# Head-size-8 cross attention without the unread products of steps 5, 7 and 9

## The reference

```python
def _attn(x, ctx, wq, wk, wv, wo, bo, heads):
    b, n, _ = x.shape
    j = ctx.shape[1]
    dh = wq.shape[1] // heads
    scale = dh ** (-0.5)
    q = (x @ wq).reshape(b, n, heads, dh).transpose(0, 2, 1, 3)
    k = (ctx @ wk).reshape(b, j, heads, dh).transpose(0, 2, 1, 3)
    v = (ctx @ wv).reshape(b, j, heads, dh).transpose(0, 2, 1, 3)
    sim = jnp.einsum('bhid,bhjd->bhij', q, k) * scale
    a = jax.nn.softmax(sim, axis=-1)
    out = jnp.einsum('bhij,bhjd->bhid', a, v)
    out = out.transpose(0, 2, 1, 3).reshape(b, n, heads * dh)
    return out @ wo + bo
h1 = _ln(x, n1_g, n1_b)
x = _attn(h1, h1, q1, k1, v1, o1_w, o1_b, heads) + x
h2 = _ln(x, n2_g, n2_b)
x = _attn(h2, context, q2, k2, v2, o2_w, o2_b, heads) + x
```

## Time and profile before

| | us |
|---|---|
| median of 3 runs | 3592.56 |
| lowest and highest | 3588.77, 3592.84 |
| the profiled execution | 3591.85 |
| its span, first to last instruction | 3590.0 |

### The profile page before, as it was taken

The page is one execution under the profiler, slowest core; times in us unless marked ns, Lnnn a source line. Parts: engine busy times, 40 slices in busy tenths (PEclk is TensorE's granted clock), DMA queues, the critical chain, the costliest instruction groups (busy, mean ns, idle before and its releaser), DMA issues. The chain is left out here.

```text
span 3590.0 us, 93153 instructions
## 1 busy us (share of the span) xinstructions
PE 3523.7 (98%) x37535; PEld 3076.2 (86%) x37535; DVE 2304.3 (64%) x3902; ACT 2078.7 (58%) x5150; POOL 1254.3 (35%) x1278
## 2 busy tenths in 40 slices
PE   8999999999999999999999999899999999999999
PEld 6777777877887999999999999788888888888888
DVE  5888866664454676676667667566666666666554
ACT  4777777775335666565656656455555555555343
POOL 4433333332442433333333333333322332233432
PEclk9999999999999999999999999999999999999999
DMA  4444433231001000000000000100000000000000
GB/s 104 112 113 99 107 77 95 77 91 56 21 0 36 2 1 2 2 1 2 2 2 1 2 2 2 27 3 3 4 3 4 3 3 4 3 3 1 20 22 22
DMA packets 99741, 101.46 MB, mean 28 GB/s; under 512 B 31248, under 2 KB 74128, under 8 KB 99344
## 3 DMA queue, kind: packets, MB, share of 16 engines
q1 hardware_dynamic: 93408, 94.41, 10.3%
q0 software_dynamic: 5120, 1.35, 0.2%
q10 hardware_dynamic: 816, 0.08, 0.0%
HBM read 20.76 MB, written 5.24 MB: 7 GB/s over the span
## 5 line engine op out<-in xcount | busy, mean ns | idle before, releaser
L1217 POOL TENSOR_TENSOR a_probs<-a_probs,a_rsums 128x1024 f32<-128x1024 f32 x160 | 303.7, 1898 | 709.1 <-DVE a_rsums L1346 707.1
L1249 ACT ACTIVATE a_probs<-a_scores_banks,a_negmax 128x128 f32<-128x128 f32 x1280 | 372.5, 387 | 197.4 <-DVE a_negmax L1325 197.4
L1729 ACT ACTIVATE c_probs<-c_scores_banks,c_negmax 128x77 f32<-128x77 f32 x1280 | 317.5, 350 | 251.7 <-DVE c_negmax L1836 251.6
L1691 POOL TENSOR_TENSOR c_probs<-c_probs,c_rsums 128x616 f32<-128x616 f32 x160 | 197.7, 1236 | 725.0 <-DVE c_rsums L1848 724.9
L731 ACT ACTIVATE s_probs<-s_scoresT_banks 128x1024 f32<-128x1024 f32 (+1 forms) x320 | 327.4, 1023 | 182.8 <-PE s_scoresT_banks L908 180.5
L817 DVE TENSOR_REDUCE s_negmax<-s_scores_banks 128x8 f32<-128x1024 f32 (+1 forms) x320 | 322.3, 1007 | 134.6 <-PE s_scores_banks L890 130.5
L1354 DVE COPY a_probsT<-a_scores_banks 128x1024 f32<-128x1024 f32 x160 | 195.7, 1223 | 169.7 <-PE a_scores_banks L1422 169.6
L2230 DVE SCALAR_TENSOR_TENSOR f_hidden<-f_value_bank,bias,f_gate 128x512 f32<-128x512 f32 x160 | 120.0, 750 | 245.2 <-ACT f_gate L2205 243.2
L686 POOL DMA_DIRECT2D s_q_stack<-s_shift x160 | 93.6, 585 | 490.2 <-ACT s_shift L754 483.8
L2205 ACT ACTIVATE f_gate<-f_gate_bank,bias 128x512 f32<-128x512 f32 x160 | 110.0, 688 | 259.8 <-PE f_value_bank L332 259.7
L1853 DVE COPY c_probsT<-c_pt_banks 77x1024 f32<-77x1024 f32 x160 | 194.5, 1216 | 77.1 <-PE c_pt_banks L1929 77.1
(11 more groups left out here) (309 smaller groups left out, 10349.5 us busy)
## 6 DMA issues: line engine op xcount, KB each, us to landing
s_q_stack<-front SPq DMA_DIRECT2D x192, 160.0 KB, 3.3
s_k_stack<-front SPq DMA_DIRECT2D x96, 160.0 KB, 3.8
s_out<-s_heads SPq DMA_DIRECT2D x128, 80.0 KB, 2.5
s_k_stack<-front SPq DMA_DIRECT2D x96, 96.2 KB, 2.8
x_tokens<-in_x SPq DMA_DIRECT2D x16, 320.0 KB, 3.7
out_x<-x_tokens SPq DMA_DIRECT2D x16, 320.0 KB, 2.4
s_q_stack<-s_shift POOLq DMA_DIRECT2D x160, 8.0 KB, 2.5
s_ctx_in<-in_ctx SPq DMA_DIRECT2D x16, 115.5 KB
```

What stands on the lines that cost most here:

```text
L1217: nc.gpsimd.tensor_tensor(probs[n % 4][:], probs[n % 4][:], rsums[n % 2][:].unsqueeze(2).broadcast_to([P, UNIT, TOK]), ALU.mult).then_inc( ...
L1249: last_one = nc.scalar.activation(probs[n % 4][:, h, :], scores[n % 2][:, h // GROUP, h % GROUP * TOK:(h % GROUP + 1) * TOK], ACT.Exp, bia ...
L1691: nc.gpsimd.tensor_tensor(probs[i][:], probs[i][:], rsums[(k - 1) % 2][:].unsqueeze(2).broadcast_to([P, UNIT, NK]), ALU.mult).then_inc(s_p ...
L1729: done = nc.scalar.activation(probs[i][:, h, :], scores[:, h // GROUP, h % GROUP * NK:(h % GROUP + 1) * NK], ACT.Exp, bias=negmax[k % 2][: ...
```

## The change

The table `KEEP` loses its entries for the steps 5, 7 and 9:

```diff
@@ -489,7 +489,7 @@
     HALF = D // 2
     SPREAD = 4
     ST_LAG, PV_LAG = 5, 6
-    KEEP = {2: 3, 4: 3, 5: 4, 6: 3, 7: 4, 8: 6, 9: 4}
+    KEEP = {2: 3, 4: 3, 6: 3, 8: 6}
     BURST, BURST_QUADS = 12, (18, 23, 28)
     CONSTANTS, CONSTANTS_ALL = 8, 17
     START, START_KEEP = 10, 4
```

## The result

The changed kernel takes 3797.4 us in the median (3780.57 to 3832.99, 4 runs) against 3592.7 us before: a ratio of 1.0578, with an interval of 1.0533 to 1.0622. The forecast was 3575.5 us. Leaving out 188 products that nobody reads costs 205 us.

A forecast was written before the change was run, and what follows sets the result against it. TensorE's own work was taken to bound the kernel. Steps 5 and 7 were to give 16.6 us and step 9 0.5, so 3592.56 - 17.1 = 3575.5 us, with a range of 3568 to 3592.

The forecast's parts named there:

- What bounds the kernel: Cross attention, 450 to 850 us: TensorE's own work sets the pace, busy 397.22 of 400 us, except at one wait.
- The price of four products: Four unread products in a step of the cross attention: 0.52 us by their starts, 0.13 us each.
- Steps 5 and 7: Cross-attention quads: nothing takes the place of the removed time in these two steps, 32 x 0.52 = 16.6 us gained.
- rival (d): Steps 6 and 8: removed time returns as waits for ScalarE or VectorE; 3584 us if half is lost; chance 0.10.
- Step 9: End of the quad: transposes wait for ScalarE's copy, so no gain in 14 quads, about 0.5 us in the fifteenth group.
- The clock: End of step 9, 0.7 us of waiting: at most two drops in the likeliest case, 1.56 us each.
- two rivals: Clock drops at step 9 in some quads, 3580 to 3592.5 us, chance 0.25; or twice per quad, 3625 us, 0.08.
- Rival (b): Clock drops twice per quad, at step 9 and between steps 5 and 8: 32 x 1.56 = 50 us, 3625 us; chance 0.08.
- The point of decision: Clock drops in the cross attention: break-even at 11, slower by over 0.2% from 16 on, one per quad.
- The range: Whole kernel's time: from full gain, 3568 us, to eleven drops of the clock, 3592 us.

## Why the prediction was wrong

**What bounds the kernel**: right. TensorE sets the pace, and at full clock the time follows its instructions.

**The price of four products**: 0.52 us was read from starts; the step got 0.45 shorter, since the product behind them costs 0.07 more when it follows the products with the values directly. The estimate from the Trainium skill's weight load, 0.43 us for four by "TensorE: Matmul & The Clock Gate", section "LDWEIGHTS (loading the stationary operand)", comes closer to this net price than my reading did. No run here shows that the loads set it.

**Steps 5 and 7**: 1.04 us per quad forecast, 0.75 measured (25.27 to 24.52). Besides the 0.07 twice, the steps 6 and 8 lose 0.15 us, in step 8 to ScalarE's copy of the heads. I had checked that copy against ScalarE's own next task, but not against TensorE's products with the values, which wait for it. This is rival (d) in small. With the products of step 9 kept, the gain was 14.2 us in the median, against the 16.6 forecast for these two steps; its interval just includes none.

**Step 9**: right that its products hide in the wait and give no time; the wait went to 0.64 us. This is where the reasoning stopped short. A piece of work that costs nothing can still be what holds the clock.

**The clock**: the step that failed. The sum of 3575.5 puts the loss of the clock at nothing, on the ground that the place lies between a case that fell and one that didn't. In the cross stage that term came to about 213 us. The place was named (the end of step 9 as the barest), and given 0.33 in two rivals with a price of 1.56 us per fall and a break-even at 11 falls. The profiled execution has five in the stage, and they cost 213 us. The price per microsecond was about right, 1.56 / 3.41 = 0.46 against 0.42. The mis-sized term is the length: I took the 3.4 us of the one fall that I had looked at the earlier trace rows, which ended at once, for the length of any. Both falls in the earlier trace rows are that long, so nothing there warned. The falls at the changed place last 51 to 307 us, since the stage at half clock wins the clock back only now and then. The second error was to ask for gaps. The prediction weighed a wait of 0.7 us against one of 1.83. The run with 31-row products fell with TensorE busy for 99.8% of the time ahead of it. The prediction also read the Trainium skill ("TensorE: Matmul & The Clock Gate", section "HAM oscillation — how this bites in real kernels") as leaning against the change. The waits of the kernel that the Trainium skill tells of there are DMA waits of about 3 to 5 us, far longer than the 0.64 us here, so it bore less on the case than that. And the wait of 0.55 us at 446.74, in the trace of before, was a case nearer than those of the earlier trace rows.

**Rival (b)**, slower, was right in sign and wrong in its mechanism: not two short falls in each quad but a few long ones. The point of decision was wrong with it: at 0.42 us for each microsecond one fall of 41 us takes the forecast gain of 17.1.

**The range** went from full gain to eleven short falls. With what the runs showed it should have held two separate cases: about 3592.7 - 12 = 3581 us if the clock holds, and the measured 3781 to 3833 if it doesn't.

## What to carry to other kernels

Before taking work off TensorE that "only" keeps it warm, ask for each place whether the work stands in the barest piece of the loop, and test removals one place at a time: here the four products that were free in time were needed to hold the clock, and of the eight that cost time ten executions showed no need. Needed isn't the same as enough: with seven products in step 9 and none in the even steps three of four executions lost the clock. Price a loss of the clock with two cases, held and lost, and not as a count of short falls: a stage that only just holds the full clock need not win it back at half. Look at the granted clock by stretches; the busy share was 98% in both kernels.

## What the runs showed of the hardware that was not expected

- TensorE stayed at 1.2 GHz for up to 369 us while it was busy for all of the time (368.60 of 368.60), in the variant with bursts in step 5.
- Four products on 31 of 128 rows, of the same length in time as full ones (0.67 and 0.68 us for four), don't hold the clock where the full ones do: 3758 us against 3593.
- In the changed kernel the falls of the stage begin within 2 us behind the start of the transposes. The long ones end 10 to 12 us behind the transposes that begin a slow quad, where the projections run, but not in every quad, and the last of them ends with the stage; why one ends after 10 us (in the variant with two products in step 9) and another after 307 stays open.
- The same instructions gave a fall of 3.4 us in one execution (before, at 100.05) and of 34 us in another (the changed kernel, at 97.7), in the self attention, behind the same wait of 1.83 us.
